# Denominator runs of three tiles in place of runs of two in the first attention of a two-layer graph network

## What is computed

```python
def _L0_gnn_ref(x, adj, W, b, att_l, att_r):
    x_l = (x @ W + b).reshape(N, NHEADS, C)                  # 4096, 8, 64
    alpha_l = jnp.einsum('nhc,hc->nh', x_l, att_l)
    alpha_r = jnp.einsum('nhc,hc->nh', x_l, att_r)
    scores = alpha_l[:, None, :] * alpha_r[None, :, :]
    scores = jnp.where(adj[:, :, None] > 0, scores, NEG_INF)
    att = jax.nn.softmax(scores, axis=1)
    out = jnp.einsum('ijh,jhc->ihc', att, x_l)
    return jax.nn.relu(out.reshape(N, NHEADS * C))

x = _layernorm(x + _L0_gnn_ref(x, adj, W, b, att_l, att_r), axis=-1)
x = _layernorm(x + _L1_gnn_ref(x, x2, v, adj), axis=-1)      # q.k attention, same mask
```

## Time and profile before

| | us |
|---|---|
| median of 3 runs (lowest and highest) | 3744.48 (3743.8 to 3744.56) |
| profiled execution | 3745.04 |
| its span, from the first to the last instruction | 3743.1 |
| TensorE busy | 3551.1 |
| VectorE busy | 2909.1 |
| ScalarE busy | 2525.6 |
| GpSimd busy | 1569.5 |

### The profile page before, as it was taken

One profiled execution on the slowest core, in us unless ns is written; L12 is line 12 of the kernel. 1 busy time (PEld: TensorE's weight loads), 2 busy tenths in 40 slices (PEclk: granted clock), 3 DMA queues, 4 the chain that ended last, 5 costly groups with the idle time before them and its releaser, 6 DMA issues. The chain is left out here.

```text
span 3743.1 us, 58557 instructions
## 1 busy us (share of the span) xinstructions
PE 3551.1 (95%) x22661; PEld 1448.4 (39%) x22661; DVE 2909.1 (78%) x2948; ACT 2525.6 (67%) x2430; POOL 1569.5 (42%) x1157
## 2 busy tenths in 40 slices
PE   6888899999999999987699999999999999999987
PEld 4665222222222222225344444444444444444434
DVE  5555899999999999977577777777777777777768
ACT  3444899999999999963466666666666666666642
POOL 3333010010010101011267666767666677667661
PEclk9999899999999999995699999999999999999995
DMA  7887677677777776667699999999999999999987
GB/s 259 298 299 245 153 161 165 152 160 156 162 160 161 154 160 153 153 157 254 174 198 198 205 205 201 208 197 199 204 205 200 205 201 198 205 202 203 191 188 247
DMA packets 375357, 729.43 MB, mean 195 GB/s; under 512 B 31376, under 2 KB 219792, under 8 KB 358720
## 3 DMA queue, kind: packets, MB, share of 16 engines
q0 software_dynamic: 99504, 419.90, 57.7%
q1 hardware_dynamic: 241552, 272.26, 23.8%
q10 hardware_dynamic: 34048, 33.82, 2.7%
HBM read 263.54 MB, written 59.69 MB: 86 GB/s over the span
## 5 line engine op out<-in xcount | busy, mean ns | idle before, releaser
L1130 DVE TENSOR_TENSOR a_weights<-a_psS,maskT 128x1024 f32<-128x1024 f32 x1024 | 1205.5, 1219 | 463.5 <-ACT a_psS L1095 463.5
L1095 ACT ACTIVATE a_psS<-a_psS,a_shift 128x1024 f32<-128x1024 f32 x1024 | 1071.4, 1084 | 678.8 <-PE a_psS L1023 678.7
L538 DVE TENSOR_TENSOR g_weights<-g_weights,maskT 128x1024 f32<-128x1024 f32 x1024 | 1169.7, 1218 | 117.5 <-ACT g_weights L525 117.5
L525 ACT ACTIVATE g_weights<-al_bc,g_shift,g_xl 128x1024 f32<-128x1024 f32 x1024 | 1167.9, 1228 | 88.4 <-PE g_psD L563 88.4
L1023 PE MATMUL a_psS<-a_q,a_k 128*64 128x512 f16 x8192 | 971.6, 380 | 17.0 <-DMA a_k<-k_scratch 15.5
L1040 PE MATMUL a_psO<-a_weights,a_v 128*64 128x512 f32 x4096 | 961.2, 592 | 0.0
L554 PE MATMUL g_psO<-g_weights,g_xl 128*64 128x512 f32 x4096 | 924.1, 598 | 23.2 <-DVE g_weights L538 23.2
L1153 POOL TENSOR_TENSOR a_pool_total<-a_pool_total,a_weights 128x1024 f32<-128x1024 f32 x336 | 924.3, 2751 | 0.0
L1023 PEld LDWEIGHTS a_psS<-a_q,a_k 128*64 128x64 f16 x8192 | 463.4, 110 | 647.0 <-issue 300.4
L1161 POOL DMA_DIRECT2D a_dma_total<-a_weights x480 | 467.1, 973 | 399.6 <-DVE a_weights L1130 202.5
L554 PEld LDWEIGHTS g_psO<-g_weights,g_xl 128*64 128x64 f32 x4096 | 277.9, 137 | 660.5 <-issue 530.8
(11 more groups left out here) (121 smaller groups left out, 1451.0 us busy)
## 6 DMA issues: line engine op xcount, KB each, us to landing
a_dma_total<-a_weights POOLq DMA_DIRECT2D x512, 512.0 KB, 5.4
g_total<-g_weights POOLq DMA_DIRECT2D x128, 1024.0 KB, 7.7
adj_sb<-in_adj_dram SPq DMA_DIRECT2D x128, 512.0 KB, 5.9
g_xl<-xl_scratch SPq DMA_DIRECT2D x128, 260.0 KB, 6.7
a_k<-k_scratch SPq DMA_DIRECT2D x256, 128.0 KB, 5.4
a_v<-in_L_gnn_v_dram SPq DMA_DIRECT2D x128, 256.0 KB, 3.9
al_bc<-alpha_scratch SPq DMA_DIRECT2D x16, 1024.0 KB, 6.7
f_oT<-o_scratch SPq DMA_DIRECT2D x16, 1024.0 KB, 6.8
```

What stands on the lines that cost most here:

```text
L525: nc.scalar.activation(w[:, u % RING, h, :], al_bc[:, g % 2, h, :], ACT.Exp, bias=shift_bc[:, g % 2, h:h + 1], scale=xl[:, slot, u % KB, 2 ...
L538: nc.vector.tensor_tensor(w[:, u % RING, h, :], w[:, u % RING, h, :], maskT[:, j, (g // PAIRS) * IC:(g // PAIRS + 1) * IC], ALU.mult).then ...
L1095: nc.scalar.activation(psS[n % RING][:], psS[n % RING][:], ACT.Exp, bias=shift_bc[:, g % 2, h:h + 1], scale=SCALE).then_inc(exped, 1)
L1130: nc.vector.tensor_tensor(w[:, u % NP, h, :], psS[n % RING][:].rearrange("p a c -> p (a c)"), maskT[:, j, (g // PAIRS) * IC:(g // PAIRS + ...
```

## The change

Two runs of three tiles take the place of three runs of two. Tiles 0, 2 and 3 are summed behind values of tile 3, and tiles 4, 6 and 7 behind values of tile 7. The function that tells ScalarE which value of `summed` to wait for follows the new table. Tiles 1 and 5 go by DMA as before, and the pass over `total` stays.

```diff
-        COUPLES = {2: (0, 2), 4: (3, 4), 7: (6, 7)}
+        RUNS = {3: (0, 2, 3), 7: (4, 6, 7)}
...
         def summed_by(u):
 
-            return u // JB * len(COUPLES) + sum(j < u % JB for j in COUPLES) + 1
+            return u // JB * len(RUNS) + sum(j < u % JB for j in RUNS) + 1
...
                 values(u)
-                if j % JB in COUPLES:
-                    for t in COUPLES[j % JB]:
+                if j % JB in RUNS:
+                    for t in RUNS[j % JB]:
                         of = u - j % JB + t
                         ins = denominators(g, w[:, of % RING, :, :], first=(of % NT == 0))
                     ins.then_inc(summed, 1)
```

## The result

The changed kernel takes 3840.62 us (median of 5 runs, 3839.95 to 3842.03) against 3743.8 for the kernel before (5 runs, 3742.11 to 3744.56). The ratio is 1.0262, with a 95% interval of 1.0248 to 1.0276: **slower by 97 us**. The forecast was 3849, in a range of 3822 to 3869. The profiled execution took 3842.03 us, with a span of 3840.1, against 3745.04 and 3743.1.

The account below looks back on a forecast made before the run. TensorE was taken to bound the kernel before, a loop through ScalarE, VectorE and TensorE the changed one. Sixteen groups at 6.54 us more gave +105 on 3744.5, so 3849 us, range 3822 to 3869.

Parts of the forecast that it names:

- The run's price: TensorE's denominator runs in the first attention: each costs 0.29 us beyond its passes, whatever number of tiles it sums.
- Rival 3: Denominator runs: cost grows with their tiles, 0.44 us a run of three, nothing saved, 3868 us; chance 4%.
- The saving of 19 us: First attention: one run of three removed in each of 64 blocks, 0.29 us each, with nothing in the way.
- The loop: Ring slots through ScalarE, VectorE and TensorE: late release stalls TensorE, half block 10.80 us against 9.73 unhindered; chance 79%.
- the 3.75 us: First attention: time from an exponential's start to TensorE's first load of that tile, made of 1.27, 1.135, 1.22 and 0.12.
- the 105 forecast: First attention: sixteen groups, each 86.4 us against 79.85 before, 6.54 us more, so +105 us.
- the bounds that the prediction gave this unknown: TensorE's wait for a mask at full clock: no signal time gives -13 us, twice it +13; 3836 to 3862.
- The group's end: Half block behind a group's end: release comes 0.86 us ahead, before the total's passes, so the half lasts 9.94 us.
- What was costed at nothing: First attention: ScalarE's take of a group (1.38 us), DMA release of tiles 1 and 5, g_xl loads; no added time.
- Rival 1: First attention: slots come free early enough, TensorE stays the bound, 19 us less, 3726 us; chance 5%.
- Rival 2: First attention: stalls lower TensorE's clock, slow halves of 19.0 us, 3931 to 4111 us; chance 4%.
- Rivals 4 and 5: First attention: stalls partly vanish, 0.4 us a half, 3804 us (6%); or gain and stalls cancel, nothing measurable (2%).

Follow-up runs that it names:

- the runs of one: The kernel before, with six runs of one tile a block, each right behind its values, in place of three runs of two: 3797.76 us, ratio 1.0147.
- the early signal: The changed kernel with `summed` raised after each tile's denominators and not at the run's end, TensorE's order unchanged: 3726.17 us, ratio 0.9954 to the kernel before.
- the kernel with runs of four and two: The changed kernel with tiles 0, 2, 3, 4 summed behind values 4 and tiles 6, 7 behind values 7: 3951.13 us, ratio 1.0556 to the kernel before.

## Why the prediction was right, point by point

- **The run's price**, 0.29 us, and that it goes with the run and not with its tiles: shown, by the runs of one (0.28 each) and by the run of three in the profile after, 1023.54 - 1020.83 = 2.71 us where 2.72 was expected. Rival 3 falls. The saving of 19 us is real: the early signal gets 17 of them.
- **The loop**: shown. Each link has its row. The halves of 10.74 (10.80 forecast) shorten with the release by just its advance and end at 9.73.
- **The size**. The term that was mis-sized is the 3.75 us from an exponential's start to TensorE's load of its tile, taken from the start of the stage. In the loop it is 3.69: VectorE's second half ends at about 1014.27 + 1.135 + 1.22 = 1016.62, and the load comes 0.07 behind it, not 0.12. That is 0.06 us in each of 112 halves and about as much at the group ends, 7.7 us in all, the difference between the 105 forecast and the 97 measured. (The other 0.7 us between 3849 and 3841 is the median of the kernel before, 3744.5 in the prediction and 3743.8 beside the result.) It lies inside the bounds that the prediction gave this unknown. The profile after has 3.75 at the start of the stage again (388.92 - 385.17). TensorE stands at its lower clock there, 0.85 us a pass, and at 1.00 in the loop; whether that is the reason was not tried.
- **The group's end**: forecast 9.94, measured 9.88, by the same 0.06. A group from release to release takes 85.9 us, against 86.4 forecast.
- **What was costed at nothing** stayed so: no wait of ScalarE for a DMA of `total` or for g_xl stands in the waits after, and the take fits where it was put.
- **Rival 1** (TensorE stays the bound) needed a loop 1.07 us shorter. The missing piece was 1.01, and making it up by an earlier release gave just the time of that rival, 3726.
- **Rival 2** (the clock) did not come with these stalls: 1.00 over the stage. Of the two rules that the prediction set against each other, both from the Trainium skill ("TensorE: Matmul & The Clock Gate"), the closing table's ("Why this matters for your kernels") agrees with this trace; the one on micro-idles between groups of matmuls ("A second HAM failure mode") does not hold for two stalls of half a microsecond in 10.7. The table's does not hold throughout either: an experiment, below, has stalls of 1.95 us, which the table still allows, and there the clock did fall in some blocks.
- **Rivals 4 and 5** (a smaller stall, or none to be measured) would have needed 0.4 and 0.9 us a half; it was 0.06.

## What to carry to other kernels

When work on a shared buffer is gathered into longer runs, price two things: the turns saved, and how old the oldest item is when its slot comes free. Count what the bound engine has ready behind the release, and hold it against the time that the producers need from release to the first new item; when the second is longer, all engines go round in a loop and none is full. Before undoing the longer run, move its signal: it may be raised as soon as the first item is done, and here that kept 17 of the 19 us saved and took the loss away.

## What was not expected of the hardware

In the kernel with runs of four and two most blocks take 23.04 us. The others take 23.33 (24.2 in three of them), and in these TensorE's clock falls behind the stall. By the length of the two tiles there, 5.35 us or more, that happens in 27 of the 64 blocks. Its matmuls, and the windows from the stall on (columns as above, clock third from the end):

```profile
1006.92 1.94 PE L554 MATMUL g_psO<-g_weights,g_xl 128*64 128x512 f32 x8
1010.81 5.35 PE L554 MATMUL g_psO<-g_weights,g_xl 128*64 128x512 f32 x16 [1.95 <-DVE g_weights L538]
1016.09 1.92 PE L563 MATMUL g_psD<-g_weights,onesF 128*32 128x512 f32 x16
1017.94 8.80 PE L554 MATMUL g_psO<-g_weights,g_xl 128*64 128x512 f32 x40
```

```profile
1007.00:1010.80 3.80, 1.86 (x8) 0.41 (x8) 2.41 (x3) 3.68 (x4) 0.00 (x0) 1.00 0.85 172
1010.80:1014.30 3.50, 3.49 (x12) 1.04 (x14) 3.50 (x4) 3.50 (x4) 0.00 (x0) 0.63 0.00 0
1034.10:1038.20 4.10, 3.73 (x16) 0.97 (x16) 4.10 (x4) 4.10 (x4) 0.00 (x0) 1.00 0.48 173
```

Between 1007.00 and 1010.80 TensorE is busy for 1.86 us and waits the rest. Behind it the granted clock of the next 3.50 us is 0.63, a mixture of 1.2 and 2.4 GHz, and two tiles take 5.35 us. A block later the same stall passes at a clock of 1.00. So behind a stall of 1.95 us, as the profile counts it, the clock sometimes fell, and with those of 0.2 to 0.3 us in the changed kernel it stood at 1.00 over the stage. What decides it from block to block stays open. The block grows by only 0.29 us, because ScalarE sets the rest of it: from the stall to the run of two takes 5.28 us here and 1178.23 - 1174.09 = 4.14 in the block shown earlier, 1.14 more, but there the tiles behind it also waited for ScalarE, 1187.81 - 1180.09 = 7.72 us for four tiles of 1.715, and here all five go through in one piece. That gives 0.86 back. What such a fall would cost where TensorE is the bound was not tried.
